# Steps of the token routing set per group, and scatters of two groups ahead of the last rstd, in a fused two-block kernel

## The reference, cut to what matters

```python
x = x + _L1_conv_ref(_ln_c(x), Wq, Wk, Wv, gamma)      # attention within each image, 576 tokens
t = t + _L1_ffn_ref(_ln_t(t), switch_w, switch_b, expert_w, expert_b)

def _L1_ffn_ref(x, switch_w, switch_b, expert_w, expert_b):
    logits = xf @ switch_w.T + switch_b                  # 16 experts
    probs = softmax(logits)
    route_probs, routes = max(probs), argmax(probs)
    pos = cumsum(one_hot(routes))[token, route] - 1      # place among the tokens of its expert
    keep = pos < capacity                                # int(1.2 * N / E)
    buf[routes, pos] = xf                                # scatter
    y = einsum('ecd,efd->ecf', buf, expert_w) + expert_b
    out = where(keep, y[routes, pos], xf) * route_probs
```

## Time and profile before

| | |
|---|---|
| median of 3 runs | 482.83 us (482.43 to 485.3) |
| profiled execution: time | 481.0 us |
| profiled execution: span, first to last instruction | 479.0 us |
| PE busy, share of the span | 376.5 us, 79% |
| DVE | 315.8 us, 66% |
| ACT | 162.4 us, 34% |
| POOL | 122.6 us, 26% |
| mean granted clock of TensorE | 0.849 |

### The profile page before, as it was taken

How to read it: one execution, slowest core, us unless ns; L and a number is a source line. 1 busy time by engine, 2 the same in 40 slices (tenths; PEclk the granted TensorE clock), 3 DMA queues, 4 the chain that set the end, 5 groups by cost and what they waited for, 6 DMA issues and landing times.

```text
span 479.0 us, 6876 instructions
## 1 busy us (share of the span) xinstructions
PE 376.5 (79%) x2123; PEld 318.9 (67%) x2123; DVE 315.8 (66%) x1009; ACT 162.4 (34%) x345; POOL 122.6 (26%) x139
## 2 busy tenths in 40 slices
PE   0875494986999999998657999998989516986961
PEld 0775493984888888887346999997889416832420
DVE  6874786777565556569566577775666632569886
ACT  2452124435223332332215455673644402300000
POOL 2333026101800000003000761101054770057710
PEclk9999755556899999999955799999998556999886
DMA  6980000000910000000021101011000118713223
GB/s 169 263 284 1 16 8 1 1 0 8 410 44 1 0 0 0 0 0 0 3 49 25 26 19 35 19 35 27 2 31 21 44 50 263 267 37 99 55 61 99
DMA packets 22905, 29.64 MB, mean 62 GB/s; under 512 B 4120, under 2 KB 18265, under 8 KB 22622
## 3 DMA queue, kind: packets, MB, share of 16 engines
q1 hardware_dynamic: 18846, 22.62, 15.5%
q0 software_dynamic: 1728, 3.54, 2.5%
q10 hardware_dynamic: 2304, 3.15, 1.8%
HBM read 13.48 MB, written 12.78 MB: 55 GB/s over the span
## 4 chain that ended last, share of the span: by engine, by line
PE 25%; DVE 15%; POOL 3%; issue 3%; ACT 3%; DMA 2%; SPq 0%; DVEq 0%; ACTq 0%
DVE R L1308 7%; PE ps L1510 7%; POOL slots L1033 3%; PE ps L1478 3%; PE ps L1623 2%; PE ps L1591 2%; PE ps L1490 2%; DVE R L1297 1%; PE ps L1497 1%; DVE mx L1110 1%; PE ps L1603 1%; DVE K L1125 1%; PE ps L1460 1%; PE ps L1459 1%; PE ps L1458 1%
## 5 line engine op out<-in xcount | busy, mean ns | idle before, releaser
L155 POOL TENSOR_TENSOR rstd<-sm,neg_half 128x9 f32<-128x9 f32 (+1 forms) x20 | 32.4, 1620 | 223.8 <-DVE sm L149 223.7
L749 PE MATMUL ps<-wide,gu_w 128*128 (+1 forms) x108 | 52.2, 483 | 2.5 <-PEq L646 2.5
L1510 PE MATMUL ps<-V,wide 128*128 128x129 f32 x400 | 53.2, 283 | 0.0
L821 ACT ACTIVATE s<-ps 128x384 f32<-128x384 f32 (+1 forms) x60 | 29.5, 491 | 68.2 <-PE ps L753 67.8
L780 PE MATMUL ps<-h,wd 128*128 128x384 f32 x120 | 50.2, 500 | 1.6 <-DVE h L865 1.2
L1510 PEld LDWEIGHTS ps<-V,wide 128*128 128x128 f32 x400 | 50.1, 198 | 0.0
L860 DVE TENSOR_TENSOR t<-ps,s 128x384 f32<-128x384 f32 x48 | 26.7, 557 | 30.7 <-ACT s L821 30.5
L1308 DVE SCALAR_TENSOR_TENSOR R<-ps,dense_w,R 128x128 f32<-128x128 f32 x144 | 37.7, 342 | 7.7 <-PE ps L1623 7.7
L1110 DVE TENSOR_REDUCE mx<-ps 128x1 f32<-128x576 f32 (+1 forms) x40 | 29.9, 751 | 12.5 <-PE ps L1478 12.3
L753 PE MATMUL ps<-wide,gu_w 128*128 (+1 forms) x108 | 37.2, 344 | 0.3 <-DVE t L860 0.3
L750 PE MATMUL ps<-wide,gu_w 128*128 (+1 forms) x108 | 37.2, 345 | 0.0
(11 more groups left out here) (196 smaller groups left out, 840.4 us busy)
## 6 DMA issues: line engine op xcount, KB each, us to landing
slots<-zrow SPq DMA_DIRECT2D x7, 768.0 KB, 8.9
xe<-slots SPq DMA_DIRECT2D x16, 192.0 KB, 5.1
slots<-wide ACTq DMA_DIRECT2D x16, 192.0 KB, 3.1
xall<-in_x SPq DMA_DIRECT2D x8, 288.0 KB, 3.5
out<-R SPq DMA_DIRECT2D x12, 192.0 KB, 2.4
Q<-sQK SPq DMA_DIRECT2D x8, 144.0 KB, 2.4
K<-sQK SPq DMA_DIRECT2D x8, 144.0 KB, 2.5
ew<-in_ew SPq DMA_DIRECT2D x1, 1024.0 KB
```

The lines of the kernel that those rows point to most:

```text
L155: nc.gpsimd.tensor_tensor(rstd[p][:rows, :n], sm[p][:rows, 5, :n], neg_half[:rows, :n], ALU.pow).then_inc(rstd_ok, 1)
L749: nc.tensor.matmul(o, gu_w[0][:, w], xTH[:, at], start=True, stop=False)
L821: nc.scalar.activation(s4[q][:r], bank[q][:r, :CH], ACT.Silu).then_inc(s_ok[q], 1)
L1510: last = nc.tensor.matmul(bank[6 + k // 3][:, k % 3 * (C + 1):(k % 3 + 1) * (C + 1)], PT[n % 2][:, jk, i0:i0 + P], V[n % 2][:, jk, :], sta ...
```

## The change

Routing and placing get their steps from two tables. Group 0 keeps steps 5 and 6; groups 1, 2 and 3 are routed at steps 6, 8, 10 instead of 7, 9, 11 and placed at 7, 9, 11 instead of 8, 10, 12. The loop is one step shorter. To make this possible the normalization on ACT moves: chunk 0 to k = 4 of the step of the statistics, chunk 1 to the end of that step, chunk 2 to k = 0 of the routing step. The moments on DVE move from the end of the step to k = 2. On POOL, three scatters of group 0 stand ahead of the rstd of group 2 and six behind it, and all scatters of group 1 stand ahead of the rstd of group 3. In a step with both, PE does the counts of one group ahead of the last transposes of the next.

```diff
-        LAST = B + 5
+        LAST = B + 4
+        ROUTER_AT, PLACE_AT = (5, 6, 8, 10), (6, 7, 9, 11)
...
+        def at_step(n, steps):
+
+            return steps.index(n) if n in steps else None
...
-            return bank[0] if c == 2 and 2 * g + 5 > B else bank[4 + c % 2]
+            return bank[0] if c == 2 and 2 * g + 4 >= B else bank[4 + c % 2]
...
                 rstd6(0)
                 rstd6(1)
-                scatter(0, range(GT))
+                scatter(0, range(SPLIT))
                 rstd6(2)
-                scatter(1, range(0, SPLIT))
+                scatter(0, range(SPLIT, GT))
+                scatter(1, range(GT))
                 rstd6(3)
-                scatter(1, range(SPLIT, GT))
                 scatter(2, range(GT))
...
+                            if k == 2:
+                                norm_moments(d, ins, GT, stats % 2, P, EPS_C if n in (0, 1) else EPS_T,
+                                             var5 if n in (0, 1) else var6, mean=0.5 if n in (0, 1) else -0.5)
-                        if k == 2 and behind(n, 5) is not None:
-                            add_bias(behind(n, 5), 0)
-                            add_bias(behind(n, 5), 1)
+                        if k == 2 and at_step(n, ROUTER_AT) is not None:
+                            add_bias(at_step(n, ROUTER_AT), 0)
+                            add_bias(at_step(n, ROUTER_AT), 1)
...
-                    if stats is not None:
-                        norm_moments(d, ins, GT, stats % 2, P, EPS_C if n in (0, 1) else EPS_T,
-                                     var5 if n in (0, 1) else var6, mean=0.5 if n in (0, 1) else -0.5)
...
+                def apply6(g, c):
+                    if c == 0:
+                        act.wait_ge(rs6, 2 * g + 2)
+                        if g == NG - 1:
+                            act.wait_ge(pv, NB_SS * (B - 1))
+                        elif g >= 2:
+                            act.wait_ge(sc6[g % 2], 16 * GT * (g // 2))
+                        else:
+                            act.wait_ge(t_ps, 3 * (g + 3))
+                    for t in range(3 * c, 3 * c + 3):
+                        ins = nc.scalar.activation(xn_buffer(g)[:, t, :], R[:, GT * g + t, :], ACT.Identity,
+                                                   bias=nmr[g % 2][:, t:t + 1], scale=rstd[g % 2][:, t:t + 1])
+                    ins.then_inc(xn6, 1)
...
+                        if k == 0 and at_step(n, ROUTER_AT) is not None:
+                            apply6(at_step(n, ROUTER_AT), 2)
...
+                        if k == 4 and behind(n, 3) is not None:
+                            apply6(behind(n, 3), 0)
...
+                    if behind(n, 3) is not None:
+                        apply6(behind(n, 3), 1)
...
-                    g = behind(n, 5)
+                    g = at_step(n, ROUTER_AT)
...
+                        if k == 4 and at_step(n, PLACE_AT) is not None:
+                            counts(at_step(n, PLACE_AT))
                         if k == (4 if n < B else 1) and g is not None:
                             router_transposes(g, 2)
-                        if k == 4 and behind(n, 6) is not None:
-                            counts(behind(n, 6))
```

More of the change, by code:

```diff
@@ L1276, in _ @@
                         low_row(n + 1)
-                    if behind(n, 6) is not None:
-                        place_sums(behind(n, 6))
-                        place_index(behind(n, 6))
-                    if behind(n, 5) is not None:
-                        add_bias(behind(n, 5), 2)
+                    if at_step(n, PLACE_AT) is not None:
+                        place_sums(at_step(n, PLACE_AT))
+                        place_index(at_step(n, PLACE_AT))
+                    if at_step(n, ROUTER_AT) is not None:
+                        add_bias(at_step(n, ROUTER_AT), 2)
                     if n > -2:
@@ L1343, in router_copy @@
                     nc.scalar.activation(router_in(g, c)[:], l_bank(g, c)[:, :CH], ACT.Copy).then_inc(l_xt, 1)
+                def apply6(g, c):
[11 more added lines that the diff above has]
+                    ins.then_inc(xn6, 1)
                 for n in range(-3, LAST):
-                    g = behind(n, 4)
                     for k in range(NB_SS):
@@ L1361, in _ @@
                                                  ACT.Copy, scale=konst[:, K_SGN:K_SGN + 1]).then_inc(sh_ok, 1)
-                        if k == 1 and behind(n, 5) is not None:
-                            router_copy(behind(n, 5), 0)
-                            router_copy(behind(n, 5), 1)
-                        if k == 1 and behind(n, 6) is not None:
-                            p = behind(n, 6) % 2
-                            act.wait_ge(d6, behind(n, 6) + 1)
-                            nc.scalar.activation(lx[p][:], lx[p][:], ACT.Exp).then_inc(ex6, 1)
-                        if g is not None and k < 3:
-                            if k == 0:
-                                act.wait_ge(rs6, 2 * g + 2)
-                                if g == NG - 1:
-                                    act.wait_ge(pv, NB_SS * (B - 1))
-                                elif g >= 2:
-                                    act.wait_ge(sc6[g % 2], 16 * GT * (g // 2))
-                                else:
-                                    act.wait_ge(t_ps, 3 * (g + 3))
-                            for t in range(3 * k, 3 * k + 3):
-                                ins = nc.scalar.activation(xn_buffer(g)[:, t, :], R[:, GT * g + t, :], ACT.Identity,
-                                                           bias=nmr[g % 2][:, t:t + 1], scale=rstd[g % 2][:, t:t + 1])
-                            ins.then_inc(xn6, 1)
+                        if k == 0 and at_step(n, ROUTER_AT) is not None:
+                            apply6(at_step(n, ROUTER_AT), 2)
+                        if k == 1 and at_step(n, ROUTER_AT) is not None:
+                            router_copy(at_step(n, ROUTER_AT), 0)
+                            router_copy(at_step(n, ROUTER_AT), 1)
+                        if k == 1 and at_step(n, PLACE_AT) is not None:
+                            p = at_step(n, PLACE_AT) % 2
+                            act.wait_ge(d6, at_step(n, PLACE_AT) + 1)
+                            nc.scalar.activation(lx[p][:], lx[p][:], ACT.Exp).then_inc(ex6, 1)
                         if k == 3 and 0 <= n < B:
@@ L1394, in _ @@
                         nc.scalar.activation(K[(n + 1) % 3][64:65, :SS], psum[1][0:1, :SS], ACT.Copy).then_inc(mH, 1)
-                    if behind(n, 5) is not None:
-                        router_copy(behind(n, 5), 2)
+                    if at_step(n, ROUTER_AT) is not None:
+                        router_copy(at_step(n, ROUTER_AT), 2)
                     high_halves(n)
+                    if behind(n, 3) is not None:
+                        apply6(behind(n, 3), 1)
                 def store(e):
@@ L1520, in router_transposes @@
                         banks_empty()
-                    elif c == 2 and 2 * g + 5 > B + 2:
+                    elif c == 2 and 2 * g + 2 >= B:
                         pe.wait_ge(lg_ok, 3 * g)
```

6 lines of the change are left out of this document (3 added, 3 removed).

## The result

The changed kernel took 495.19 us (median of 4 runs, 494.19 to 498.66), the kernel before 482.63 beside it (481.8 to 485.3): a ratio of 1.0265, 95% interval 1.0211 to 1.032. It is 12.6 us slower; the forecast was 490.8, with 484.5 to 495.5 as its range.

The account below looks back on a forecast made before the run. The start of group 2's last scatter was taken to bound the kernel, with 85.0 us rigid behind it. It moves from 394.0 to 402.2, +8.2; on the runs' 482.6 that gives 490.8 us, range 484.5 to 495.5.

Parts of the forecast that it names:

- Step 3, the K row, +0.8: Three normalizations of group 0 moved onto ACT delay the K row's copy by 0.8 us (bounds 0 and 0.9).
- Step 6, +2.9: Group 1's routing beside group 0's placing makes group 0's slots 2.9 us later; first scatter at 354.0, not 351.09.
- Step 7 gives everything back: Without its routing, step 7 lets PE begin image 7's first attend at 362.2, against 362.24 before.
- POOL and ACT, 370.5: With rstd among them, group 0's scatters all land by 370.5, and only then can ACT write group 2.
- Step 8: PE waits for ACT until 374.1 amid image 7's attends; then 8.8 us at mixed clock, group 3's statistics path ready at 382.9.
- From there to the slots, 8.0: After step 8, statistics, moments, routing and placing take 8.0 us, so sidx is ready at 390.9.
- Last scatter 10.2 behind the first: Group 2's scatters start at 391.2 and the last 10.2 us later, at 401.4, or 402.2 with step 3's 0.8.
- The last 85 us are rigid: From the start of group 2's last scatter to the end, 85.0 us remain unchanged, with the same instructions in both kernels.
- Rival C: Clock stays at 1.2 GHz throughout step 8 and the placing: +3.5 on top, 494.3 us; chance 0.10.
- Rival B: A draw: PE's idling is smaller and group 2's first scatter starts at 383 to 386; about 483.5 us; chance 0.10.
- Rival D: PE takes ready attends past the waiting transposes, so step 8 has no stall: 478 us; chance 0.08 together with A.
- Rival A: Six scatters, up to 7.6 us, are won if group 0's land before about 363: 475.2 us; chance 0.08 with D.

Follow-up runs that it names:

- e10: Changed kernel with group 2 normalized into a buffer of its own, in a quiet session: 485.29 us, ratio 1.0116 to the kernel before.
- e3: Changed kernel with group 2 normalized into a buffer of its own, in a session with the kernel before at 504.39: 512.4 us, ratio 1.0182.
- e8: Changed kernel with the placing's sums and index on DVE ahead of the low half of the K row: 493.69 us, ratio 1.0192 to the kernel before.
- e7: Kernel before with only POOL's new order of scatters and rstd, all steps kept: 488.14 us, ratio 1.0105 to the kernel before.
- e6: Changed kernel with own buffer for group 2, its transposes and logits behind image 7's attends, and earlier placing: 484.07 us, ratio 1.0033 to the kernel before.
- e3b: Changed kernel with group 2 normalized into its own buffer, repeated with the kernel before at 506.38: 515.0 us, ratio 1.0218.

## Why the prediction was right, and where its sizes were off

The direction, the mechanism and the order of the steps were right: the slower kernel, POOL idle for 1.60 (about 2 forecast), ACT released by the scatters, PE idle ahead of the transposes (5.13, where I had 6 or more), statistics of group 3 late, the last group's scatters released by `sidx`. e10 shows that this wait is the larger part: with it gone, 1.5 of the 2.65% are back. 490.8 was 4.4 too low, inside the range, and that is partly luck, for its errors cancelled in part and the largest of them (step 7) had no effect. By its steps:

- *Step 3, the K row, +0.8*: the insertion cost 0.83, as forecast: from the exponential ahead of it to the copy of the K row it is 1.82 (303.52 to 305.34), before 0.99 (303.92 to 304.91). But the changed program was 0.40 ahead there, so the row came only 0.43 later.
- *Step 6, +2.9*: the count of instructions was right, TensorE's level was left out. The first scatter started at 357.78, not 354.0 (354.8 with step 3's 0.8). With all of step 6 at full level, as in e3, the routing costs 3.0; the half level adds 3.2. In the changed kernel the granted clock was 0.51 from 336.5 to 340 us and 0.53 from 350 to 353, and two attends took 2.35 and 2.36 instead of 1.28.
- *Step 7 gives everything back*: it didn't, and my sum didn't say so either. Its terms (5.6, 1.5, 1.4, 0.6, 1.1) add to 10.2, which from 353.2 gives 363.4 and not 362.2. Image 7's first attend began near 367.9 (an estimate: ten of the 30 products of 3.60 from 366.75 belong to image 6), against 362.24 before. Most of that is the late end of step 6; one more attend, at 357.55, took 2.35 at a granted clock of 0.50. The late start did little harm, for PE waited for ACT from 370.35 to 375.48 anyway. The moments of group 2, ready at 363.1 instead of 359.5, are late with step 6, since DVE's statistics began at 358.48 and not 354.7.
- *POOL and ACT, 370.5*: 374.17. The form (moments, rstd, six scatters, landing) held. The 2.9 over 371.3 (370.5 with step 3's 0.8) are those of step 6, handed on by the moments.
- *Step 8*, from ACT's start to the statistics 12.4: measured 11.98 (374.17 to 386.15). The mixed level that I chose between all-high and all-low was right, ten products at 2.36 and twenty at 2.48. That the mixture came out so was partly luck: in e8 the whole of step 8 ran at half level and the same stretch took 15.7.
- *From there to the slots, 8.0*: 7.4 (386.15 to 393.59). *Last scatter 10.2 behind the first*: 10.18.
- *The last 85 us are rigid*: this failed. 89.2, with the same instructions. In the other profiles it was 85.4 (e8), 87.8 (e7), 88.4 (e6) and 84.5 (e10), and it doesn't follow the place of the last scatter (406.73, 398.61, 395.78 and 396.39 in that order). Where it is long, dense products ran below full level: a group of twelve takes 5.42 or 7.11 to 8.40. With one profile a kernel, it stays open whether these 4 us belong to the kernel or to the run; the four times of the changed kernel alone spread over 4.5. The medians grew by 2.5 more than the last scatter's delay in the changed kernel, 1.9 more in e10, 0.6 more in e7 and 0.6 less in e6.

So +10.1 instead of +8.2 up to the last scatter (+2.9 by step 6, -0.4 by step 8, -0.6 on the way to the slots), and +4.2 instead of 0 behind it. Rival C, the clock, had about the right quantity (3.5) in the wrong place: 3.2 of it came in step 6 and not in step 8, and part of the tail may be the same. Rival B fell with the 7.50 of ACT. Rival D fell with the 5.13: PE did not take a ready attend past the waiting transposes. Rival A's own condition, group 0's scatters landed by 363, was not met (374.1). Its prize was also smaller than I had written: by the estimate above the slots of group 1 leave 1.0 of the 7.6, and in e6 and e10, where PE's stall is gone, the last scatter is still later than before.

Two rows I read wrongly, without harm to the sum. The 40 records from 362.24 are four attends of image 7, not all five; the fifth stands at 367.21. And the landing of 3.6 for the last scatter of group 0 before has no tie to the rstd behind it (last section).

## What to carry to other kernels

When a group is moved a step earlier in a hand-written pipeline, look first whether its result is earlier at all: the step that takes it in may grow by what the other gives back. Then ask of each instruction that is moved up which buffer it writes and who reads that last; here an in-order engine carried one late release of a buffer through three others. An order among queues is safe only together with the order on the engines that wait for it: e7 has the reordering without the step that makes it harmless, and pays 1%.

## What the runs showed of the hardware that I had not expected

- TensorE can be at half level in dense work, shortly after pauses of about 1 us. In the changed kernel PE idled 1.24 ahead of 334.74, worked densely at a granted clock of 1.00 until 336.5, and stood at 0.51 from there to 340.0; ten attend products took 2.35 there, and 1.28 in the same program elsewhere. The kernel before had the same pause of 1.24 ahead of 334.28 and stayed at 1.00. The same kernel can go either way: e3 and e3b stayed at full level in step 6, e10 didn't, which is worth 3.2 us. The mean granted clock of the whole span doesn't show this (0.896 for the changed kernel against 0.849 before, although it lost time there). What decides between the two is open.
- A scatter mostly lands 2.2 us after its start, but not always: the last of group 0 took 3.6 in the kernel before, and in the changed kernel the fifth of group 0 took 3.3 with scatters on both sides of it. A computation of POOL behind the scatter doesn't cause this by itself: the scatters at 372.71 before and at 382.79 in e10 have an rstd behind them and landed after 2.2. Before, the 3.6 made ACT start at most 0.6 later (365.14, with `nmr` done at 364.59), so it hid at most 0.6 of the cost of the new order.
- In some sessions DVE, ACT and PE stop for 4 to 18 us while POOL's indirect transfers run, and the same kernel takes 4% longer. The profile names no releaser for it; its cause is open.
